# Expert block: 32 more fixed rows per expert in tiles shared by four neighbours, own-weight half tiles only beyond 288 rows, no laps, early reads of five picks

## What is computed

```
logits = x @ gate_w.T
topv, topi = jax.lax.top_k(logits, TOP_K)              # TOP_K = 8 of E = 64
rw = jax.nn.softmax(topv)
W = zeros((N, E)).at[arange(N)[:, None], topi].set(rw)
gu = jnp.einsum('nh,eih->nei', x, gu_w)                # gate and up, 2 x 128
gate, up = (gu[..., :I], gu[..., I:])
inter_w = jax.nn.silu(gate) * up * W[:, :, None]
out = jnp.einsum('nei,ehi->nh', inter_w, dp_w)
out = out + sh_g * sh_out                              # shared expert
x = x + gb * out
```

## Time and profile before

| | |
|---|---|
| three runs | 968.95, 970.89, 973.75 us (median 970.89) |
| span of the profiled execution | 965.6 us |
| the profiled execution's own time | not listed apart; the median of the runs is 5.3 us above its span, which is what lies around it |
| PE busy in the span | 872.5 us, 90% |
| DVE, POOL, ACT | 48%, 48%, 22% |
| moved by DMA | 221.36 MB, mean 229 GB/s |

### The profile page before, as it was taken

How to read it: one execution, slowest core, us unless ns; L and a number is a source line. 1 busy time by engine, 2 the same in 40 slices (tenths; PEclk the granted TensorE clock), 3 DMA queues, 4 the chain that set the end, 5 groups by cost and what they waited for, 6 DMA issues and landing times.

```text
span 965.6 us, 12358 instructions
## 1 busy us (share of the span) xinstructions
PE 872.5 (90%) x3437; PEld 514.2 (53%) x3437; DVE 465.5 (48%) x1177; ACT 214.3 (22%) x559; POOL 458.7 (48%) x447
## 2 busy tenths in 40 slices
PE   6999989989988694979989998999999999986997
PEld 2434534534534343657666665666666666763442
DVE  4797785788586540423323323333233333324496
ACT  2022221321312111212232222322223222321000
POOL 1420055236355766357556666566665656655000
PEclk9999999999998697989999999999999999998999
DMA  9951003103003152788898998889998997899997
GB/s 341 326 163 71 1 8 96 45 2 104 1 1 115 41 190 73 229 289 277 289 322 272 339 323 315 307 286 338 325 319 302 311 333 262 283 354 402 382 419 315
DMA packets 76927, 221.36 MB, mean 229 GB/s; under 512 B 19078, under 2 KB 19462, under 8 KB 76472
## 3 DMA queue, kind: packets, MB, share of 16 engines
q1 hardware_dynamic: 48760, 149.12, 43.9%
q0 software_dynamic: 28096, 71.42, 21.0%
HBM read 183.98 MB, written 48.87 MB: 241 GB/s over the span
## 4 chain that ended last, share of the span: by engine, by line
PE 60%; issue 8%; DVE 7%; another core or an unknown queue 7%; DMA 4%; SPq 3%; ACT 2%; ACTq 0%; POOL 0%; DVEq 0%; POOLq 0%
PE bank L2026 17%; PE bank L2046 8%; PE bank L1798 7%; PE bank L2016 5%; PE bank L1845 5%; PE bank L1911 3%; PE bank L2136 3%; DMA front<-y_rows 3%; PE bank L2037 2%; PE bank L1809 2%; SPq L668 2%; PE bank L2054 1%; PE bank L1930 1%; DMA front<-h_rows,gid_fixed 1%
## 5 line engine op out<-in xcount | busy, mean ns | idle before, releaser
L2026 PE MATMUL bank<-h2T,wqkv 128*128 128x256 f32 x1024 | 243.1, 388 | 9.9 <-issue 9.6
L719 POOL DMA_INDIRECT slot_table<-pair,place x128 | 130.4, 1019 | 183.3 <-DVE place L1262 118.2
L2026 PEld LDWEIGHTS bank<-h2T,wqkv 128*128 128x128 f32 x1024 | 193.1, 194 | 41.1 <-issue 16.5
L775 POOL DMA_INDIRECT y_rows<-front,tbl x110 | 113.6, 1033 | 83.8 <-DVE front L1641 38.1
L766 POOL DMA_INDIRECT front<-h_rows,gid_fixed x112 | 115.8, 1034 | 69.1 <-issue 31.6
L2046 PE MATMUL bank<-wqkv,front 128*128 128x512 f32 x256 | 127.9, 621 | 11.2 <-DVE front L1622 7.5
L1641 DVE TENSOR_SCALAR front<-bank,wgt 128x512 f32<-128x512 f32 x146 | 107.1, 748 | 43.3 <-DMA y_rows<-front,tbl 19.8
L1006 ACT ACTIVATE h2T<-bank 128x512 f32<-128x512 f32 x148 | 82.2, 595 | 161.4 <-issue 65.6
L1798 PE MATMUL bank<-wqkv,front 128*128 128x512 f32 x256 | 113.5, 594 | 0.0
L1622 DVE TENSOR_TENSOR front<-bank,front 128x256 f32<-128x256 f32 x64 | 27.2, 424 | 177.4 <-ACT front L1016 135.2
L2016 PEld LDWEIGHTS bank<-const,front 128*128 128x128 f32 x592 | 69.1, 143 | 62.0 <-issue 47.4
(11 more groups left out here) (292 smaller groups left out, 860.1 us busy)
## 6 DMA issues: line engine op xcount, KB each, us to landing
wqkv<-in_experts SPq DMA_DIRECT2D x64, 768.0 KB
front<-in_experts SPq DMA_DIRECT2D x36, 512.0 KB
front<-y_rows SPq DMA_DIRECT2D x20, 768.0 KB, 12.4
front<-in_experts SPq DMA_DIRECT2D x36, 256.0 KB
wqkv<-y_rows SPq DMA_DIRECT2D x12, 768.0 KB, 13.4
front<-in_w_mod SPq DMA_DIRECT2D x5, 1024.0 KB, 10.1
x<-in_x SPq DMA_DIRECT2D x4, 1024.0 KB, 10.8
h_rows<-h SPq DMA_DIRECT2D x4, 1024.0 KB
```

What stands on the lines that cost most here:

```text
L719: pool.indirect_dma_start(out=slots[:, :], out_offset=bass.IndirectOffsetOnAxis(ap=place[b % 2][:, i, k:k + 1], axis=0), in_=pair[:, b * T ...
L775: pool.indirect_dma_start(out=y_rows[:, :], out_offset=bass.IndirectOffsetOnAxis(ap=to, axis=0), in_=yb[s], in_offset=None, bounds_check=P ...
L2026: mm = pe.matmul(pair_bank[u % 2][:, j * PAIR:(j + 1) * PAIR], w[:, at:at + INNER], xT[u % 2][:, k, :], start=(k == 0), stop=(k == KC - 1))
```

## The change

Every expert gets 32 more fixed places, so 288. They lie in 16 *group* tiles: each has 32 rows of each of four neighbouring experts, works with their weights, which are still in their slots, and loads none. It uses PE in four column parts of 32. Seven rest tiles (14 halves of 64 rows) remain, for experts beyond 288 rows. There are no laps: all 64 pairs stand in the body, which has 151 tiles in 87 units: 64 pairs, 16 groups, 7 rests. A loop for what nothing else holds (`used > 0`) is skipped for this data.

The other edits: seven weight slots (and two more at first, which then serve the rests), so nine experts' weights are read at the start, and then four at once after a group tile's down; the parts of the slot table read without waiting for the first downs; the rest tiles' row numbers fetched by seven more indirect DMAs; the weight per row of a single tile picked by DVE (L1644) and not by ACT; `turn_inter` of a single ahead of the next unit's gate-up, and its down right behind that; five picks read early instead of two, in 20 chunks of 1 MB at fixed tiles of the loop's last third (`CHUNK_AT`, L690, L693), the second to fifth pick through two chunk buffers that DVE adds up (L1675, 56 adds in the loop and 8 after it) while SP waits on `s_added` for the buffers; three picks read late, in 16 reads of 768 KB (L739) through eight buffers, all three summed by PE (L2201).

```
-WSLOTS = 4
+WSLOTS = 7
+FIRST_SLOTS = 9
-REST = 18
-REST_AFTER = [22 + 2 * (42 * m // 17) for m in range(REST)]
+CAP = FIXED * P + QUARTER
+GROUP_AFTER = [7, 9] + [GROUP * (i + 1) for i in range(2, GROUPS)]
+REST_AFTER = [18, 22, 26, 30, 34, 38, 42]
-BACK = 5
-EARLY = 2
+BACK = 8
+EARLY_UPTO = [44, 52, 56, 60, 60]
+EARLY = len(EARLY_UPTO)
+CHUNK_AT = [EARLY_TILES[0] + 1 + 3 * i for i in range(CHUNKS)]
+CHUNK_AT += [EARLY_TILES[1] + 1 + 2 * i for i in range(CHUNKS)]
+CHUNK_AT += [EARLY_TILES[2] + 1 + 2 * i for i in range(CHUNKS)]
+CHUNK_AT += [EARLY_TILES[3] + i for i in range(2 * CHUNKS)]
...
+            def read_chunk(j):
+                k, c = j // CHUNKS, j % CHUNKS
+                landed_upto(sp, EARLY_TILES[k])
+                if k:
+                    n = j - CHUNKS
+                    if n >= ECHUNKS:
+                        sp.wait_ge(s_added, CHUNK * (n - ECHUNKS + 1))
+                    for i in range(CHUNK):
+                        sp.dma_start(next_row[CHUNK * (n % ECHUNKS) + i], y_view[CHUNK * c + i, :, TOPK - 1 - k, :]).then_inc(s_next[n % ECHUNKS], 16)
...
+            for t in range(BODY_TILES):
+                if t in GROUP_TILE:
+                    sp.wait_ge(s_d, t + 1)
+                    i = GROUP_TILE.index(t)
+                    for e in range(GROUP * i + 1, GROUP * (i + 1) + 1):
+                        if next_in_slot(e):
+                            load_fixed(next_in_slot(e))
...
-            def gate_up_rest(u):
-                n = REST_UNIT.index(u)
-                if n:
-                    pe.wait_ge(s_iT, n)
+            def gate_up_single(u):
+                m = SINGLE_UNIT.index(u)
+                if m:
+                    pe.wait_ge(s_iT, m)
+                if SINGLE[m][0] == "rest":
+                    pe.wait_ge(s_rest_gu, 32 * (SINGLE[m][1] + 1))
                 pe.wait_ge(s_xT, UNIT[u][0] + 1)
                 for k in range(KC):
-                    for h in HALVES:
-                        mm = pe.matmul(rest_bank[rows_of(h), 0:GU], xT[u % 2][:, k, rows_of(h)], rest_w[h][:, k * GU:(k + 1) * GU],
-                                       start=(k == 0), stop=(k == KC - 1), tile_position=(0, h * HALF_TILE))
+                    for rows, at, w in parts_of(m):
+                        mm = pe.matmul(rest_bank[rows, 0:GU], xT[u % 2][:, k, rows], w[:, k * GU:(k + 1) * GU],
+                                       start=(k == 0), stop=(k == KC - 1), tile_position=(0, at))
...
+            for u in range(UNITS):
+                if u + 1 < UNITS:
+                    turn(u + 1)
+                if u - 1 in SINGLE_UNIT:
+                    turn_inter(u - 1)
...
+                if u in SINGLE_UNIT:
+                    gate_up_single(u)
...
+                    gate_up(u, slot_of(u))
+                if u:
+                    downs(u - 1)
```

More of the change, by code:

```diff
@@ L240, in build @@
[L240 to L248, removed]
+        halves = sb("halves", [EV, 1])
@@ L273, in build @@
-        early = [early[k * TILES:(k + 1) * TILES] for k in range(EARLY)]
-        assert all(len(e) == TILES for e in early)
+        act = [small[:, i * PAIR:(i + 1) * PAIR] for i in range(2)]
+        inter = [small[:, (2 + i) * PAIR:(3 + i) * PAIR] for i in range(RING)]
+        yb = [r[:, 2 * i:2 * i + 2, :].rearrange("p a c -> p (a c)") for r in (kcos, ksin) for i in range(2)]
+        fixed_w = [store[:, at:at + WROW] for at in SLOT_AT]
+        rest_w = fixed_w[WSLOTS:]
+        back = [w.rearrange("p (k d) -> p k d", k=LATE) for w in fixed_w[:BACK]]
@@ L1652, in lists @@
+            ADD_AT = [CHUNK_AT[CHUNKS + m // CHUNK] + SOON + m % CHUNK // 2 for m in range(CHUNK * ADDED)]
             def lists(t):
@@ L1684, in _ @@
+                gated(u)
+                if UNIT[u][0] == ID_AT + REST + 5:
+                    list_rest()
+                taken(u)
+                while added < CHUNK * ADDED and ADD_AT[added] <= UNIT[u][-1]:
+                    add_next(added)
+                    added += 1
+            take_inter(UNITS - 1)
+            taken(UNITS)
+            while added < CHUNK * ADDED:
+                add_next(added)
+                added += 1
             used = laps_used(ve)
-            for r in range(OWN_LAPS):
-                lap(r)
@@ new lines, in down_single @@
+            def down_single(u):
+                t, m = UNIT[u][0], SINGLE_UNIT.index(u)
+                if SINGLE[m][0] == "rest":
+                    pe.wait_ge(s_rest_down, 32 * (SINGLE[m][1] + 1))
+                pe.wait_ge(s_iT, m + 1)
+                pe.wait_ge(s_y, t - 1)
+                for rows, at, w in parts_of(m):
+                    mm = pe.matmul(bank[4 + t % 2][rows, :], inter[u % RING][:, P + at:P + rows.stop], w[:, KC * GU:WROW],
+                                   start=True, stop=True, tile_position=(0, at))
@@ L2096, in body, with downs @@
+            def downs(u):
+                if u in SINGLE_UNIT:
+                    down_single(u)
+                else:
+                    down(u, slot_of(u))
+            pe.wait_ge(s_shi, BATCH)
+            turn(0)
+            for u in range(UNITS):
+                if u + 1 < UNITS:
+                    turn(u + 1)
+                if u - 1 in SINGLE_UNIT:
+                    turn_inter(u - 1)
                 if u == 0:
@@ L2124, in _ @@
+                    gate_up(u, slot_of(u))
+                if u:
+                    downs(u - 1)
+            turn_inter(UNITS - 1)
+            downs(UNITS - 1)
             used = laps_used(pe)
-            for r in range(OWN_LAPS):
-                lap(r)
-            with pe.If(used > OWN_LAPS):
-                with pe.Fori(OWN_LAPS, LAPS) as r:
+            with pe.If(used > 0):
+                with pe.Fori(0, COLD) as r:
                     with pe.If(r < used):
-                        lap(r)
```

1098 lines of the change are left out of this document (547 added, 551 removed).

## The result

The changed kernel takes 1021.66 us (1011.09 to 1029.4, four runs) against 972.27 of the kernel before on the same chip: a ratio of 1.050, 95% interval 1.045 to 1.055. The prediction, 955 us with a range of 928 to 1000, was wrong in its sign. The ratio leaves out the longest of the four, 1029.4, a slow run. Times of the kernel before differ by chip (958 to 972 us in the experiments), so each experiment is given by its ratio to the kernel before on the same chip; 0.01 of that ratio is about 10 us. A price read from a trace is of one execution.

A forecast was written before the change was run, and what follows sets the result against it. Loop bound by PE with little DMA room, tail by bytes. Span 965.6 + 14 − 6 − 31 + 8 = 950.6 us; with 5.3 from span to median 956, stated as 955, range 928 to 1000.

The forecast's parts named there:

- Moved into the loop: Expert loop's last third, tiles 106 to 150: 12.6 MB more early reads +6 and DVE adds +2, together +8 us.
- rival C: Tiles 142 to 149: chunks through two buffers make SP's queue 19 us late; no change, 966 to 979 us; chance 0.15.
- All singles: Group and rest tiles in the loop: 23 at 4.83 us, 111 us against 97 for 18 before, +14.
- the sign given: Expected in the changed kernel's profile: PE idle before the turn of inter, about 1.4 us × 23.
- rival B: Turn of inter after each single: the late signal leaves 2.1 us bare; slower, 985 to 1017 us; chance 0.22.
- A group tile's PE work: Group tiles in the loop: gate-up 1.88 us, down 1.06, with transposes and turn 3.5 us, a rest tile's price.
- The tail: After the loop: 16 reads (12.6 MB) remain of 32, 32 us at 392 GB/s, −31 us.
- Laps: End of the expert loop: 8 pairs took 54.6 us, should take 48.4 without listing and register waits, −6.
- Start: Start, 362 to 425 us: nine weights instead of four come in where DMA is at 0.57; 0, bounds −10 and +5.

The follow-up runs named there:

- 32 transposes: The changed kernel with 32 more transposes on PE, once, behind unit 2 of the loop, their result unused: ratio 1.058 to the kernel before.
- late turn: The changed kernel with a single's turn of inter put back behind the next unit's gate-up, its down one unit later: 1028.55 us, ratio 1.062.
- the order alone in the kernel before: The kernel before with one line moved, a rest's turn of inter ahead of the next unit's gate-up: 996.36 us against 958.17, ratio 1.039.

## Why the prediction was wrong

Of the 70 us between the forecast span and the measured one, most lie in the chunks and in the price of a few singles. What the forecast had at nothing, a lower clock behind some of PE's stands, runs through both.

**The term that failed most was "Moved into the loop": +8, with DVE's adds at +2.** Leaving the reads and adds out gave 35 to 39 us. The step took the landing time as bandwidth, at most 10 us, and the adds as 0.7 us each ahead of a product. It did not add up the chain of one chunk: scatter landed, issue, landing, against the two tiles of the schedule. That is 16 us against 6. The prediction had part of this as rival C, with its 19 us of SP's queue and 31 in all, but placed it at tiles 142 to 149 alone and gave it 0.15. It began at the second pick's first chunk, at 846 us, and cost 20 us in the loop and 18 at its end. The 18 are what rival C meant by a queue that is 19 us late; that DVE would stand in the middle of the loop was in none of the cases. The same bytes on another schedule, with a third buffer, gave 22 us back, so the waits and not the bytes made more than half of it.

**"All singles": 4.83 us each, mis-sized.** For the 14 of the steady part it was 5.6 (78.3 / 14), so the forecast was 11 us too low; with other edits it was 4.7 (32 transposes) and 6.2 (late turn). The mechanism, bare signals behind an early turn, is shown by the order alone in the kernel before: 1.5 to 2.1 us per rest tile, the clock included, against 1.4 by the step.

In the changed kernel PE stood 35.8 us before its 23 turns of inter, 1.6 each, where the sign given was 1.4; among the 14 it is 17.7 us, nearly all at the groups. What the step left out there is the clock (5 us of the 11) and that even a rest with its signal in time costs 3.77 us, not 3.47 (4 us). That the average of the stands came out so near is partly luck. The step has silu start some 3 us after the gate-up's end, taken from the mean wait of 4.2 us. But a wait of ACT does not start with the gate-up: in the earlier trace rows silu starts 5.9 us after that end, and over the 18 rests of that trace 1.3 to 6.9 us after it, 4.6 in the mean. By 4.6 the same working gives 2.4 us bare and not 1.4; rival B's 4.9 is too small in the same way. The early turn is not a debt that the old order pays off in the changed kernel, as the late turn showed.

For the first three groups the step failed outright: 35.8 us for 14.5, +21. Their signals are late in chains of three, the first two gate-ups take 12 us more than 1.93 each would, and the clock costs some 7; these overlap. Moving the fetches of row numbers moved part of it; what makes the rest stays open. The last five, chunks left out, cost 30.7 for 24.2, +6.

**"A group tile's PE work", 3.5 us: right for most.** In 12 of the 16 group tiles the gate-up takes 1.9 to 2.0 us, so column parts work abreast with their loads, as the front's row had shown. In two it takes 2.4 to 2.5, and in the first two 7.8 and 8.0. By the rule of the Trainium skill ("TensorE: Matmul & The Clock Gate", Part 3, The mechanism), that a weight load overlaps running matmuls only where the row groups differ, no group's would work abreast so. The trace disagrees: in the first group's gate-up 23 of the loads lie within 1.01 us, less than half of what they would take one after another at the 0.106 us of the earlier trace rows.

**"The tail", −31: right in size (−32), and for another reason in part.** PE and not DMA now sets it, so that the number of bytes gave the right time is partly luck. **"Laps", −6, and "Start", 0:** the laps went. The way to the first single, over its pairs, took 4.5 us less, from a first gate-up that starts 1.4 later: 3 back.

The forecast added 5.3 us to its span for what lies around it. On record, where a run has both, the difference is 1.8 to 3.2 us; so some 2 to 3 of the 5.3 were the spread between executions, which changes nothing here.

Predicted span 950.6, measured 1020.5: 70 more. Of it the chunks are 29.5 (the 37.5 found in the prices, less the 8 forecast), the first three groups 21, the steady singles 11, the last five groups 6.5, the end without chunks 5 (59.9 for the 55.1 that the terms give: 87.3 less a pair, plus a single, less 31), and the start gives 3 back.

**Open:** what holds PE's signals back. The silus start 1.2 to 7 us after the end of their matmuls, and several signals come at once within 0.2 us. Empty instructions and the burst of weight loads did not move it. Half the instructions in a group's gate-up did, and so did 32 real transposes upstream, in one kernel and not in the other, but in both cases the other prices rose. Nor is it known why the first two gate-ups come in pieces, or whether signals would be late without the records of a profile. No run took the clock apart from the waits that it follows; its share is worked out from the granted levels.

## What to carry to other kernels

A read that depends on a scatter has three durations in a row, the scatter's landing, the issue and its own landing; place its consumer by their sum, or on an engine or at a place in the queue where nobody stands behind it. Where a producer's signal is known to come late, the work between producer and consumer is what pays for it: moving a wait ahead of one gate-up cost 2.1 us per rest tile in the mean, and 4 where the signal was late. A stand of PE costs more than its length: behind one of 3.5 us the granted clock was 0.50 for 3.4 us, which cost 1.8 more. So look at the granted clock of each stretch before its time is put down to waits alone. A new kind of unit is priced by the waits around it, and these moved with edits elsewhere, so a price of 5 us was good to ±1 at best.

## Not expected of the hardware

Sixteen and 32 column-tiled instructions took the same 1.9 us, but the 32 of the first two group tiles took 8. Five signals of PE arrived within 0.2 us at 596.2 us, the first of them 5.3 us after its gate-up's end and the last 2.7 us after PE had done all that it had. And 32 transposes, some 140 us ahead, removed the late silu waits among 14 later tiles (seven waits, 39.4 us, to none) without making the kernel faster.
